# Latent attention: the softmax reciprocals move from TensorE transposes to a scaling of the probabilities by GpSimd

## The reference, cut to what matters

```python
q = rmsnorm(x @ Wq_a, q_norm_w) @ Wq_b          # 16 heads of 128 + 64
kv = rmsnorm(x @ Wkv_a, kv_norm_w) @ Wkv_b      # keys and values of 16 heads
q_rot, k_rot = apply_rope(q_rot), apply_rope(x @ Wk_rope)
scores = einsum('bqhd,bkhd->bhqk', qf, kf) * 192 ** -0.5
p = softmax(where(causal, scores, min), axis=-1)
o = einsum('bhqk,bkhd->bqhd', p, v).reshape(B, T, 2048) @ Wo
```

## Time and profile before

| | |
|---|---|
| median of 3 runs | 3301.82 us (3297.91 to 3304.41) |
| the profiled execution's own time | 3297.91 us |
| its span in the trace | 3295.8 us |
| TensorE matmul / VectorE / ScalarE / GpSimd busy | 3187.0 / 2411.4 / 1952.9 / 828.0 us |
| call 0 of the latent attention, in the trace | up to about 488 us |
| call 1 | about 1925 to 2387 us |
| granted TensorE clock, mean | 0.994 |

### The profile page before, as it was taken

One profiled execution on the slowest core, in us unless ns is written; L12 is line 12 of the kernel. 1 busy time (PEld: TensorE's weight loads), 2 busy tenths in 40 slices (PEclk: granted clock), 3 DMA queues, 4 the chain that ended last, 5 costly groups with the idle time before them and its releaser, 6 DMA issues. The chain is left out here.

```text
span 3295.8 us, 89322 instructions
## 1 busy us (share of the span) xinstructions
PE 3187.0 (97%) x34218; PEld 2636.1 (80%) x34218; DVE 2411.4 (73%) x7923; ACT 1952.9 (59%) x4769; POOL 828.0 (25%) x828
## 2 busy tenths in 40 slices
PE   8999989999999999999999969999899999999999
PEld 6888878888888888888888857888777777777787
DVE  5777778787778878787877647777766777777764
ACT  3565556666666666666666625555565556555653
POOL 2333322232223323222222223333300111111100
PEclk9999999999999999999999989999999999999999
DMA  6000000000000000000000040000000000000000
GB/s 245 1 1 1 1 14 21 22 22 19 21 12 25 18 25 19 22 15 22 22 22 21 9 165 1 1 1 1 1 1 1 2 1 1 1 5 4 5 8 11
DMA packets 51337, 66.83 MB, mean 20 GB/s; under 512 B 4962, under 2 KB 40291, under 8 KB 49379
## 3 DMA queue, kind: packets, MB, share of 16 engines
q1 hardware_dynamic: 49330, 60.21, 5.7%
q10 hardware_dynamic: 1584, 0.93, 0.1%
HBM read 58.56 MB, written 2.56 MB: 19 GB/s over the span
## 5 line engine op out<-in xcount | busy, mean ns | idle before, releaser
L1433 DVE SCALAR_TENSOR_TENSOR d_acc<-d_raw,d_taps,d_acc 128x255 f32<-128x255 f32 x1116 | 623.7, 600 | 128.9 <-ACT d_raw L1421 115.7
L2496 ACT ACTIVATE s_probs<-s_probs,s_nmax 128x128 f32<-128x128 f32 (+1 forms) x768 | 286.9, 446 | 176.1 <-DVE s_nmax L202 175.4
L1688 ACT COPY d_power<-bank 128x768 f32<-128x768 f32 x320 | 259.1, 810 | 135.1 <-PE bank L1681 135.1
L202 DVE CUSTOM_DVE_ANT_0 s_probs<-bank,mask 128x128 f32<-128x128 f32 (+1 forms) x768 | 225.4, 348 | 101.9 <-PE bank L2477 101.9
L736 POOL TENSOR_TENSOR a_q<-a_rope 64x512 f32<-64x512 f32 x128 | 165.9, 1296 | 527.5 <-DVE a_recip L806 312.9
L773 ACT ACTIVATE a_area<-a_area,a_nmax 128x128 f32<-128x128 f32 (+1 forms) x512 | 226.4, 443 | 87.8 <-DVE a_nmax L202 87.1
L1419 ACT ACTIVATE d_acc<-bank,d_tap_bias,d_taps 128x256 f32<-128x256 f32 x372 | 189.9, 561 | 148.4 <-PE bank L1397 138.6
L202 DVE CUSTOM_DVE_ANT_0 a_area<-bank,mask 128x128 f32<-128x128 f32 (+1 forms) x512 | 158.6, 355 | 131.9 <-PE bank L754 127.1
L801 ACT COPY a_area<-bank 128x512 f32<-128x512 f32 (+1 forms) x260 | 137.2, 581 | 111.6 <-PE bank L792 111.6
L726 DVE TENSOR_TENSOR a_rope<-bank,a_sinT 32x512 f32<-32x512 f32 x256 | 177.4, 693 | 5.6
L1836 POOL TENSOR_TENSOR d_o_rs<-d_o_var,minus_half 128x4 f32<-128x4 f32 x64 | 69.5, 1087 | 419.3 <-DVE d_o_var L1830 419.3
(11 more groups left out here) (287 smaller groups left out, 8640.1 us busy)
## 6 DMA issues: line engine op xcount, KB each, us to landing
d_alpha<-d_alpha_rows SPq DMA_DIRECT2D x64, 256.0 KB, 3.6
d_g_decay<-d_running_rows SPq DMA_DIRECT2D x32, 258.0 KB, 3.5
a_w_o<-in_a_w_o SPq DMA_DIRECT2D x2, 2048.0 KB, 16.8
a_area<-in_a_q_nope SPq DMA_DIRECT2D x2, 1536.0 KB, 9.2
x<-in_x SPq DMA_DIRECT2D x8, 256.0 KB, 15.0
d_wk<-in_d_wk SPq DMA_DIRECT2D x1, 2048.0 KB
d_wq<-in_d_wq SPq DMA_DIRECT2D x1, 2048.0 KB
d_wv<-in_d_wv SPq DMA_DIRECT2D x1, 2048.0 KB
```

Source lines behind the costliest of these rows:

```text
L202: return core.nc.vector.tensor_tensor_reduce(out=out, in0=scores, in1=core.mask[:, blocks], scale=-1.0, scalar=HIGHEST, op0=ALU.add, op1=A ...
L1433: last = nc.vector.scalar_tensor_tensor(out=convolved(G, r)[:, j, d:T], in0=raw[:, r % 2, j, 0:T - d], scalar=taps[:, r // 2, h, 3 - d:4 - ...
L1688: nc.scalar.copy(power[:], b_step[:, :, 0:3 * P]).then_inc(g.step_out, 1)
L2496: last = nc.scalar.activation(own, own, ACT.Exp, scale=-1.0, bias=nmax[:, s % 2, t, i:i + 1])
```

## The change

GpSimd multiplies the probabilities of a pair in place in SBUF with their reciprocals (`scale_pool`, two instructions: both heads' first 128 columns, both heads' other 256), and TensorE transposes probabilities that are already divided. The transposed reciprocals are gone, with their spreading, their place in `probsT`, and the product in `oT_dve`, which becomes a copy. The transposes of a pair, the product with the values, the share of the output and the residual each move behind by one slot, so that a call has 67 slots in its loops where it had 66, and the buffer of probabilities grows from 4 heads to 6.

```diff
@@ -371,12 +371,12 @@
         z, up, down, wt = (w_out[:, 2 * n:2 * n + 2] for n in range(4))
         cosT = sb("cosT", [P, T])
         sinT = sb("sinT", [P, T])
-        area = sb("area", [P, H * QL])
-        q_nope = area[:].rearrange("p (h l) -> p h l", h=H)
+        area = sb("area", [P, H * QL + 2 * T])
+        q_nope = area[:, 0:H * QL].rearrange("p (h l) -> p h l", h=H)
         probs = area[:, 0:AHEAD * SCORE_COLS].rearrange("p (a k) -> p a k", a=AHEAD)
-        probsT = area[:, AHEAD * SCORE_COLS:AHEAD * SCORE_COLS + 8 * P].rearrange(
+        probsT = area[:, AHEAD * SCORE_COLS:(AHEAD + 2) * SCORE_COLS].rearrange(
             "p (j k) -> p j k", j=2)
-        oT = area[:, H * QL - 2 * T:H * QL].rearrange("p (j t) -> p j t", j=2)
+        oT = area[:, H * QL:H * QL + 2 * T].rearrange("p (j t) -> p j t", j=2)
         t_bias = sb("t_bias", [P, 1, D])
         w_ste = sb("t_w_ste", [P, KC, D])
 
@@ -781,37 +780,32 @@
             if h == 0:
                 pe.wait_ge(g.w_out_ready, staged)
             pe.wait_ge(*g.probsT_ready(0, h - 1))
-            if n < PAIRS_ALL:
-                pe.wait_ge(*g.probs_ready(0, h + 1))
-                for b in range(3):
-                    last = nc.tensor.transpose(b_pT[j][:, b * P:(b + 1) * P],
-                                               probs[:, h % AHEAD, b * P:(b + 1) * P],
-                                               core.ident[:])
-            if n > 0:
-                pe.wait_ge(*g.recip_spread(0, n))
-                last = nc.tensor.transpose(b_pT[j][:, 3 * P:4 * P], wide_recip[:, (n - 1) % 2, j],
+            pe.wait_ge(*g.probs_scaled(0, n + 1))
+            for b in range(3):
+                last = nc.tensor.transpose(b_pT[j][:, b * P:(b + 1) * P],
+                                           probs[:, h % AHEAD, b * P:(b + 1) * P],
                                            core.ident[:])
             last.then_inc(g.probsT_in_psum.sem, 1)
 
         def transposed_act(act, n, j):
             act.wait_ge(*g.probsT_in_psum(0, 2 * n + j + 1))
             act.wait_ge(*g.pv_in_psum(0, n))
-            act.wait_ge(*g.oT_ready(0, n - 1))
-            lo, hi = (0 if n < PAIRS_ALL else 3 * P), (4 * P if n > 0 else 3 * P)
-            nc.scalar.copy(probsT[:, j, lo:hi], b_pT[j][:, lo:hi]).then_inc(g.probsT_ready.sem, 1)
+            nc.scalar.copy(probsT[:, j], b_pT[j][:, 0:SCORE_COLS]).then_inc(g.probsT_ready.sem, 1)
 
         def recip_dve(dve, n):
             dve.wait_ge(*g.probs_ready(0, 2 * n + 2))
-            dve.wait_ge(*g.recip_spread(0, n - 1))
+            dve.wait_ge(*g.probs_scaled(0, n - 1))
             nc.vector.reciprocal(recip[:, n % 2], sums[:, n % 2]).then_inc(g.recip_ready.sem, 1)
 
-        def spread_pool(pool, n):
+        def scale_pool(pool, n):
             pool.wait_ge(*g.recip_ready(0, n + 1))
-            pool.wait_ge(*g.probsT_in_psum(0, 2 * n))
-            nc.gpsimd.tensor_copy(
-                wide_recip[:, n % 2].rearrange("p t (j c) -> p t j c", j=2),
-                recip[:, n % 2].rearrange("p j (t c) -> p t j c", c=1)
-                .broadcast_to([P, NT, 2, CL])).then_inc(g.recip_spread.sem, 1)
+            at = 2 * n % AHEAD
+            for t, cols in enumerate((slice(0, P), slice(P, 3 * P))):
+                own = probs[:, at:at + 2, cols]
+                last = nc.gpsimd.tensor_tensor(
+                    own, own, recip[:, n % 2, :, t:t + 1]
+                    .broadcast_to([P, 2, cols.stop - cols.start]), ALU.mult)
+            last.then_inc(g.probs_scaled.sem, 1)
 
         def pv_pe(pe, n):
             it = n // PAIRS
@@ -831,12 +825,9 @@
 
         def oT_dve(dve, n):
             dve.wait_ge(*g.pv_in_psum(0, n + 1))
-            dve.wait_ge(*g.probsT_ready(0, 2 * n + 4))
+            dve.wait_ge(*g.probsT_ready(0, min(2 * n + 4, 2 * PAIRS_ALL)))
             dve.wait_ge(*g.y_done(0, n - 1))
-            nc.vector.tensor_tensor(oT[:, n % 2].rearrange("p (t q) -> p t q", t=NT),
-                                    b_o[:, 0:T].rearrange("p (t q) -> p t q", t=NT),
-                                    probsT[:, :, 3 * P:4 * P], ALU.mult)\
-                .then_inc(g.oT_ready.sem, 1)
+            nc.vector.tensor_copy(oT[:, n % 2], b_o[:, 0:T]).then_inc(g.oT_ready.sem, 1)
 
         def project_out_pe(pe, n):
             it, p = n // PAIRS, n % PAIRS
@@ -911,7 +902,7 @@
                 project_pe(pe, 0)
                 project_pe(pe, 1)
                 output_weights_pe(pe)
-                for n in range(PAIRS_ALL + 2):
+                for n in range(PAIRS_ALL + 3):
                     it, p = n // PAIRS, n % PAIRS
                     last_slot = n - (NB - 1) * PAIRS if after_attention else -1
                     stream_slot = n - (NB - 1) * PAIRS if not after_attention else -1
@@ -920,10 +911,10 @@
                         scores_pe(pe, n, 1)
                     if n + 2 < PAIRS_ALL:
                         project_pe(pe, n + 2)
-                    if 0 < n <= PAIRS_ALL:
-                        pv_pe(pe, n - 1)
-                    if n > 1:
-                        project_out_pe(pe, n - 2)
+                    if 1 < n <= PAIRS_ALL + 1:
+                        pv_pe(pe, n - 2)
+                    if n > 2:
+                        project_out_pe(pe, n - 3)
                     if it + 1 < NB:
                         if p == 1:
                             prep_early_pe(pe, it)
@@ -942,12 +933,12 @@
                         pe.wait_ge(*g.latT_ready(NB - 2, 2))
                         pe.wait_ge(tern.added, NB - 2)
                         opening.xnT_pe(pe, 0, 0)
-                    if n <= PAIRS_ALL:
-                        transposes_pe(pe, n, 0)
-                        transposes_pe(pe, n, 1)
+                    if 0 < n <= PAIRS_ALL:
+                        transposes_pe(pe, n - 1, 0)
+                        transposes_pe(pe, n - 1, 1)
                     if last_slot == 1:
                         opening.ab_pe(pe, 0)
-                    if last_slot >= 2:
+                    if 2 <= last_slot < PAIRS + 2:
                         opening.project_pe(pe, last_slot - 2)
                 if after_attention:
                     pe.wait_ge(tern.added, NB - 1)
@@ -997,8 +988,8 @@
                         ln_normalize_dve(core, dve, mla_at(it + 1), it + 1)
                     if ternary_in(it) is not None and p == 6:
                         ln_normalize_dve(core, dve, ternary_at(ternary_in(it)), ternary_in(it))
-                    if n > 1:
-                        oT_dve(dve, n - 2)
+                    if n > 2:
+                        oT_dve(dve, n - 3)
                     if it + 1 < NB:
                         if p == 4:
                             prep_rms_dve(dve, it)
@@ -1032,7 +1023,7 @@
                         opening.ab_dve(dve, 0)
                         opening.silu(dve, 0, 0)
                         opening.silu(dve, 0, 1)
-                    if n > 1 and p == 1:
+                    if n > 2 and p == 2:
                         residual_dve(dve, it - 1)
                 if after_attention:
                     ternary_stats_dve(dve, NB - 1)
@@ -1088,12 +1079,16 @@
                         act.wait_ge(*g.lat_in_psum(NB - 2, NT))
                         act.wait_ge(tern.y_in_psum, NB - 2)
                         opening.xnT_act(act, 0, 0)
+                    if n == PAIRS_ALL:
+                        transposed_act(act, n - 1, 0)
+                        transposed_act(act, n - 1, 1)
                     if last_slot == PAIRS:
                         opening.ab_act(act, 0)
                         opening.sigmoid_act(act, 0, 0)
                         opening.sigmoid_act(act, 0, 1)
-                    transposed_act(act, n, 0)
-                    transposed_act(act, n, 1)
+                    if 0 < n < PAIRS_ALL:
+                        transposed_act(act, n - 1, 0)
+                        transposed_act(act, n - 1, 1)
                     if last_slot == 1:
                         opening.ab_raw_act(act)
                     if 2 <= last_slot < PAIRS:
@@ -1150,8 +1145,8 @@
                             ln_rstd_pool(core, pool, ternary_at(ternary_in(it)))
                         if p == 6:
                             ternary_bias_pool(pool, ternary_in(it))
-                    spread_pool(pool, n)
-                    pool.wait_ge(*g.recip_spread(0, n + 1))
+                    scale_pool(pool, n)
+                    pool.wait_ge(*g.probs_scaled(0, n + 1))
                     if n >= (NB - 1) * PAIRS and not after_attention:
                         opening.pool(pool, n - (NB - 1) * PAIRS)
                 if after_attention:
```

More of the change, by code:

```diff
@@ L258, in __init__ @@
         self.recip_ready = sig("recip_ready", PAIRS)
-        self.recip_spread = sig("recip_spread", PAIRS)
+        self.probs_scaled = sig("a_probs_scaled", PAIRS)
         self.pv_in_psum = sig("pv_in_psum", PAIRS)
@@ L274, in __init__ @@
```

(6 more changed lines are left out.)

1 line of the change is left out of this document (removed).

## The result

The changed kernel takes 3327.77 us in the median of 4 runs (3321.05 to 3335.27), the kernel before 3299.86 (4 runs, 3295.77 to 3304.41): 1.0085 of the time, with an interval of 1.0059 to 1.0111. A second measurement, among the experiments, gives 1.0074 (1.0060 to 1.0088). So it is slower by 21 to 28 us; 34.6 was the sum of the prediction. The profiled execution took 3328.36 us, its span 3326.6, that of before 3295.8: 30.8 to explain.

The account below looks back on a forecast made before the run. TensorE (97% busy) sets the pace except where VectorE's chain does, at p = 1 and p = 6. -18.0 + 18.0 + 14.4 + 5.4 + 6.0 + 2.5 + 6.3 = +34.6 us gave 3332.5 to 3336.4, called 3334; range 3289 to 3354.

Parts of the forecast that it names:

- The transposes, 18.0 gained: On TensorE, 256 transposes go, worth 28.2 us; only 18.0 us of this was forecast to reach the end.
- the 41 slots a call: Slots where removed transposes were counted as shortening the run: 82 over both calls, at 0.22 us each.
- p = 1 and p = 6: Slots where GpSimd's products hold VectorE's L188 and TensorE then waits: 1.2 us each, 18.0 and 14.4 in all.
- p = 5: Slot where the products, ending at 127.1, delay VectorE's L602 by 0.45 us, 12 times: 5.4 us lost.
- A sequence 1.7 us longer: Expected sign: each sequence grows some 1.7 us, from 1.2 + 1.65 less five sets of transposes.
- The end of call 0: 6.0 us lost to products holding VectorE's taps and set-up; residual 6.4 us later through the extra slot to drain.
- its 2.7 for the load: At call 0's end, ScalarE's table load comes 2.7 us later, behind the copies of the last transposes.
- The end of call 1: Weight scalings held up by the products cost 2.5 us, and the extra slot to drain 1.8 us.
- The starts: At each call's start 1 us comes back, as an output share no longer lies in slot 2; 1.9 in the sum.
- the second (cheap products, +3.5): Rival: GpSimd's products take 1.2 us a pair, L188 waits 0.45, p = 5 is free; 3303 us, chance 0.08.
- the first: Rival: GpSimd's products do not hold VectorE up, so 18.0 is gained and 6.3 lost; 3288 us, chance 0.15.
- The rule that I drew from the Trainium skill: VectorE instructions with two SBUF inputs or a two-port mode wait for GpSimd's whole instruction; masked maxima and L836 stay free.

Follow-up runs that it names:

- A: Changed kernel with GpSimd's two products held back until L188 has ended, at two slots of a sequence; 3302.84 us, 1.0002 of the kernel before.
- B: Changed kernel with GpSimd's two products cut to one column of each tile, waits and order kept; 3293.20 us, 0.9969 of the kernel before.
- D: Changed kernel with ScalarE's last two copies of probabilities behind the logarithm and sigmoids again, as before the change; 3320.72 us, 1.0057 of the kernel before.
- F: Changed kernel with the edits of A and D joined; 3297.11 us, 0.9991 of the kernel before.
- G: F, with GpSimd's products also waiting for VectorE's set-up and taps in call 0's last sequence; 3294.28 us, 0.9984 of the kernel before.
- H: Changed kernel with each GpSimd product split into two one-head instructions taking the reciprocal as per-partition scalar, nothing held back; 3321.04 us, 1.0073 of the kernel before.

## Why the prediction was right, and where it was not

The direction, the mechanism and the two places were right: VectorE's L188 is held by a product on GpSimd, ends 0.14 behind it, and passes the delay to TensorE through the output's copy; A removes just this and is level with before in the median. The time, 3334, was near 3327.77 partly by luck, since terms erred in both directions:

- **The transposes, 18.0 gained.** Right for the sequences. B, without collisions, has them 1.10 us shorter; five sets of 0.22 were 1.10. No run measures the 41 slots a call by themselves.
- **p = 1 and p = 6, 1.2 us each, 32.4 in all.** Over by 60%: A puts 0.73 on each. The step that failed is the length of the pair, taken as 1.9 us: it spans 1.61 alone, 0.3 less, since 512 columns with a broadcast operand take 1.06 in the mean, not 1.21, and 256 take 0.62, not 0.68. L436, from which I took the 1.21, is a sum, and what it broadcasts is a whole tile read twice, not one column. The L188 let in between cost GpSimd 0.05 instead of 0.15, and rounding up gave the last 0.1.
- **p = 5, 5.4.** Wrong, nothing is there: the products ran from 121.21 to 122.82, and L601, at 122.70, took 0.41. The shorter pair was all but over when it came.
- **A sequence 1.7 us longer.** It is 0.38 longer: 1.47 less 1.10, rounded apart. The sum had 2.85 less 1.1.
- **The end of call 0, 6.0 for the taps and 6.4 for the slot.** 14.5 in all, and close in parts: without the collisions 5.7 less (B against the change), by D's order 3.6 less, by neither some 5. The slot's 6.4 had the chain of D in it, copies ahead of the table load and L830 behind the sigmoids, and its 2.7 for the load came true: 478.86 is 6.4 behind the earlier trace rows, of which 3.6 lie ahead of the last scores (465.57, before 461.97). From these scores the residual is 23.9 away, before 16.0: 8.0 more instead of 6.4. The missing 1.6 is TensorE at its lower clock behind the longer wait: the granted clock is 0.50 from 483.5 to 486.9, and the 5.13 us from the product with the values to the last output share are 3.49 in D, 1.64 less for the same matmuls. The sum had no term for the clock, and of the 14.5 it can be up to 5.1.
- **The end of call 1, 4.3.** 3.9 and 3.6 in the two profiles, with the clock at 0.50 for 3.4 us more than before, which can be 1.7 of it.
- **The starts, 1.9 back.** About 4 back at call 0, more than an output share explains, and the cause is open; none at call 1, where before, A, B, D, F and G all take 22.4.
- **Not in the sum:** the stretches that the change does not touch, 10.9 us in the first profile and 5.3 in the second, most of it the clock. Without them the first profile would stand 19.9 over before, and 34.6 would have been 15 too much. That 3334 lies 6 us from the measured time is therefore in part luck; the direction is not.

Of the rivals, the second (cheap products, +3.5) had the nearer value for p = 5, and the first did not occur. The rule that I drew from the Trainium skill (SBUF — State Buffer, Who interferes with whom) held as far as the prediction used it: the masked maxima kept 0.29 and 0.42 us in the 275 cases that overlap a product, and L830 its 0.42 in 47. The same section says that a VectorE instruction with two inputs in SBUF contends with any GpSimd instruction that reads SBUF; H speaks against more than a slight hold-up by the scalar-operand form: beside a rotation and that form six taps took 3.92 us, beside the rotation alone 3.69 (G), beside the rotation and the broadcast products 4.70.

## What to carry to other kernels

Before work moves to an engine with time to spare, look at what starts together with it: here GpSimd's products and VectorE's normalization stand behind the same power on GpSimd and start 0.34 us apart, at the only two places of a sequence where TensorE had no room. A wait that lets the critical instruction go first, put on the engine with slack, brought the kernel level with the one before. And where a step is moved by a slot, follow every in-order queue at the drain: at the end of call 0 one pair of copies ahead of a table load cost 3.6 us, as much as the collisions of two and a half sequences.

## What was not expected of the hardware

- GpSimd with one wide operand and a per-partition scalar hardly holds VectorE (0.83 us for 0.73, beside 3.07 us of it), with two wide operands, one of them broadcast, it does (1.47). Its price is its own length: 256 columns take 0.93 us in the scalar form and 0.62 in the broadcast form. Whether the number of operands or the other instruction is the cause was not separated.
- A product with one broadcast column takes 0.62 us for 256 columns and 1.06 for 512, where the earlier trace rows has 0.46 for 128 with two full tiles and 1.27 for 512 with a tile that is read twice.
- The start of call 1, the same code, took 22.4 us in seven profiles and 23.1, 24.8, 27.6, 30.5 and 30.6 in five others. The mean granted clock of the stretch is 1.00 in the seven and in the one with 23.1, and 0.93, 0.84, 0.75 and 0.75 in the other four, in weight products beside the loads (DMA share 0.92 in the rows shown). All five are of kernels with the change's order, but so are five of the seven, and 30.6 and 23.1 are of the same kernel, so that a link to the change is neither shown nor excluded.
- The same wait can end at either clock: at one place near the end of call 0 TensorE waited 2.90 us in F and went on at 0.50, and 2.89 us in G and went on at 1.00. At such places two profiles differ by more than the edit between them.
